# First MLP layers as Strassen block products over batches of 1024 tokens, with layer 2 added up in SBUF and attention two pairs at a time

## The reference

```python
q, k, v = x @ Wq, x @ Wk, x @ Wv
attn = softmax(q k^T * V ** -0.5)
attn_out = (attn @ v) @ Wp + bp
cms_out = gelu(attn_out @ cW1 + cb1) @ cW2 + cb2 + one_hot(target_codes, V)
modifier = gelu(concat([attn_out, cms_out]) @ mW1 + mb1) @ mW2 + mb2
x = clip(x + cms_out + modifier, 0, 1)
# expert e = stream[b] of each sequence
h = gelu(x @ W_down[e] + b_down[e]) @ W_up[e] + b_up[e] + x
out = layernorm(h) * ln_w[e] + ln_b[e]
```

## Time and profile before

| | us |
|---|---|
| median of 3 runs | 1153.08 |
| lowest, highest | 1152.85, 1154.77 |
| span of the profiled execution | 1152.9 |

### The profile page before, as it was taken

One profiled execution on the slowest core, in us unless ns is written; L12 is line 12 of the kernel. 1 busy time (PEld: TensorE's weight loads), 2 busy tenths in 40 slices (PEclk: granted clock), 3 DMA queues, 4 the chain that ended last, 5 costly groups with the idle time before them and its releaser, 6 DMA issues.

```text
span 1152.9 us, 14949 instructions
## 1 busy us (share of the span) xinstructions
PE 1119.0 (97%) x5273; PEld 935.2 (81%) x5273; DVE 519.2 (45%) x741; ACT 458.4 (40%) x739; POOL 126.2 (11%) x92
## 2 busy tenths in 40 slices
PE   8999999999999999999999999899999999899996
PEld 7888877888897887888888888688889788688885
DVE  4443354323566335322467434532346733624337
ACT  4354452333443443332444444333336244424432
POOL 1000031000005005000003201300000500500002
PEclk9999998999999998999999999999999999999999
DMA  6402354552113235473110335346311232553310
GB/s 220 172 30 92 109 174 117 185 181 81 48 36 109 78 116 151 146 254 109 55 55 9 118 106 173 96 138 243 100 36 55 71 113 76 170 137 107 104 44 37
DMA packets 135314, 128.30 MB, mean 111 GB/s; under 512 B 5950, under 2 KB 106362, under 8 KB 133242
## 3 DMA queue, kind: packets, MB, share of 16 engines
q1 hardware_dynamic: 132832, 120.61, 32.9%
q0 software_dynamic: 2368, 7.35, 1.8%
q10 hardware_dynamic: 90, 0.02, 0.0%
HBM read 119.57 MB, written 8.39 MB: 111 GB/s over the span
## 4 chain that ended last, share of the span: by engine, by line
PE 83%; issue 10%; DVE 4%; ACT 1%; POOL 1%; DVEq 0%; POOLq 0%; DMA 0%; ACTq 0%
PE bank L172 28%; PE bank L174 27%; PE bank L173 27%; DVE w_lo L616 1%; DVE hid_lo L616 1%; POOL rstd L909 1%; DVE aw_lo L616 1%; PE bank L384 0%; ACT aw_hi L511 0%; DVEq L78 0%; DVE stat L725 0%; ACT gel L446 0%; DVE x_lo L616 0%; DVE ya_lo L616 0%; DMA x_raw<-in_L_cond_Wq 0%
## 5 line engine op out<-in xcount | busy, mean ns | idle before, releaser
L616 DVE TENSOR_TENSOR w_lo<-w_raw,w_hi 128x512 fp32r<-128x512 f32 (+1 forms) x256 | 233.3, 927 | 128.2 <-ACT w_hi L437 113.8
L616 DVE TENSOR_TENSOR hid_lo<-gel,hid_hi 128x512 fp32r<-128x512 f32 x128 | 105.9, 827 | 397.9 <-ACT gel L446 397.7
L445 ACT ACTIVATE hid_hi<-bank,bias 128x512 fp32r<-128x512 f32 x128 | 88.3, 690 | 406.6 <-PE bank L174 406.6
L172 PE MATMUL bank<-hid_hi,w_lo 128*128 128x512 f32 x512 | 202.6, 396 | 15.1 <-DVE hid_lo L616 15.1
L172 PE MATMUL bank<-ya_hi,w_lo 128*128 128x512 f32 x512 | 200.8, 392 | 3.3 <-DVE w_lo L616 3.3
L173 PE MATMUL bank<-hid_hi,w_hi 128*128 128x512 f32 x512 | 202.0, 395 | 0.0
L174 PE MATMUL bank<-hid_lo,w_hi 128*128 128x512 f32 x512 | 201.9, 394 | 0.0
L174 PE MATMUL bank<-ya_lo,w_hi 128*128 128x512 f32 x512 | 200.0, 391 | 0.0
L173 PE MATMUL bank<-ya_hi,w_hi 128*128 128x512 f32 x512 | 199.8, 390 | 0.0
L437 ACT ACTIVATE w_hi<-w_raw 128x512 fp32r<-128x512 f32 x128 | 81.3, 635 | 159.7 <-PE bank L174 159.7
L172 PEld LDWEIGHTS bank<-hid_hi,w_lo 128*128 128x128 f32 x512 | 97.4, 190 | 38.7 <-DVE hid_lo L616 12.9
(11 more groups left out here) (151 smaller groups left out, 1257.0 us busy)
## 6 DMA issues: line engine op xcount, KB each, us to landing
w_raw<-in_L_cond_cW SPq DMA_DIRECT2D x128, 256.0 KB, 2.7
w_raw<-in_L_cond_mW SPq DMA_DIRECT2D x64, 512.0 KB, 4.3
w_raw<-in_L_cond_mW SPq DMA_DIRECT2D x64, 256.0 KB, 4.5
aw_hi<-proj_hi SPq DMA_DIRECT2D x6, 1024.0 KB, 7.0
aw_lo<-proj_lo SPq DMA_DIRECT2D x6, 1024.0 KB, 8.9
x_raw<-in_x SPq DMA_DIRECT2D x4, 1024.0 KB, 7.7
proj_hi<-aw_hi SPq DMA_DIRECT2D x2, 1024.0 KB, 6.0
proj_lo<-aw_lo SPq DMA_DIRECT2D x2, 1024.0 KB, 8.0
```

Of the source, the lines that this page charges most:

```text
L172: nc.tensor.matmul(dst, w_lo, a_hi, start=start, stop=False, **kw)
L445: nc.scalar.activation(hid_hi[:, q % 2, :], ps[4 + q][:, :], ACT.Gelu, bias=b)
L616: sub = lambda dst, a, hi: nc.vector.tensor_tensor(dst, a, hi.bitcast(F32), ALU.subtract)
```

## The change

Two pairs make a batch b of 1024 tokens; there are two batches. A step of the MLP is a quad, 256 hidden columns by 1024 tokens, and a batch has 24 quads in three phases of eight: phase 0 is cW1 on the attention output, phase 1 mW1's upper half on the attention output (no layer 2: its combinations, 1 MB a quad, are stored in DRAM as pre_d), phase 2 mW1's lower half on cms, to which pre_d is loaded back and added. In a quad the 512 inputs, the 256 columns and the 1024 tokens are each cut in two, and layer 1 is the seven block products of Strassen (in Winograd's form), p1 to p7, each of two `mm3` with 512 columns. Sums of weight blocks, S1 to S4, are formed on VectorE for each quad (`dve_s`) and split with A11, A12, A22 (w1_first: A11, A12, S1, S2; w1_second: A22, S3, S4; 1792 elements for high and low each); sums of token blocks, T1 to T4, once for each phase input, and split with B11, B21, B22 (`dve_t_sum`, `act_t`, `dve_t`, 1024 elements each).

ScalarE copies p1, p1+p6 and p5 out of PSUM (s1, s2, s5; in phase 2 VectorE adds them to pre: `dve_s_pre`), VectorE adds to them (c11, c22, c12 in `dve_c`), c21 is copied by ScalarE; then Gelu and hid. Quads overlap: in iteration `it` TensorE takes p1, p2, p5, p6 of quad it, p7, p4, p3 of quad it-1 and, between them, eight steps (six matmuls each) of layer 2 of quad it-2, in banks 6 and 7, which VectorE adds into `acc` in SBUF one by one (`dve_evac`). Iterations 0, 1 and 10 to 17 have no layer 2. POOL keeps only the powers of the layer norm (four columns in one); `dve_resid` adds x to acc in iteration 15, in two instructions of 2048 elements.

Attention takes both pairs of a batch one behind the other, x being copied twice by ScalarE (xf, x_hi). The expert of a batch (`pe_expert`, both pairs, down, residual and up) comes behind the next batch's attention, or at the end. Its weights come in eight pieces of 1024 elements for a batch (`load_piece`) through two buffers of `e_raw`, which are the same bytes as `w1_raw`: SyncE loads piece k when piece k-2 is split, and W1 of quad 0 of the next batch when piece 6 is split. ScalarE's order at the second entry (`act_attention`) is VectorE's below: pieces 0, 1, xp, pieces 2, 3, ao of the first pair, B11, B21, ao of the second, T1, expert down of the first pair, pieces 4, 5, xp, T2, pieces 6, 7, w1_first, T3, B22, down of the second pair, T4. All loops are unrolled.

```diff
+        def pe_mlp(pe, b):
+            def l1(i, bank, w, t, start):
+                hi, lo = (tc_hi, tc_lo) if phase_of(i) == 2 else (ta_hi, ta_lo)
+                which = phase_of(i) // 2
+                if i in (0, 1, 2 * NQ, 2 * NQ + 1):
+                    pe.wait_ge(t_lo, 14 * b + 7 * which + T_NO[t] + 1)
+                for k in range(2):
+                    last = mm3(ps[3 * (i % 2) + bank][:, :], w1_hi[:, i % 2, W_NO[w], k, :],
+                               w1_lo[:, i % 2, W_NO[w], k, :], hi[:, T_NO[t], k, :], lo[:, T_NO[t], k, :],
+                               start and k == 0, k == 1, skip_group_check=True)
+                return last
+            def first(i, which):
+                g = quad(b, i)
+                if which == 1:
+                    pe.wait_ge(w1_l1, 3 * g + 2)
+                    if i >= 2:
+                        pe.wait_ge(c21_done, g - 1)
+                    elif b == 0:
+                        pe.wait_ge(ao_done, 8)
+                    else:
+                        pe.wait_ge(z_sum, 4 * (i + 1))
+                    l1(i, 0, "A11", "B11", True).then_inc(p1_mm, 1)
+                elif which == 2:
+                    if i >= 2:
+                        pe.wait_ge(c11_done, g - 1)
+                    l1(i, 1, "A12", "B21", True).then_inc(p2_mm, 1)
+                elif which == 5:
+                    pe.wait_ge(w1_l1, 3 * g + 3)
+                    if i >= 2:
+                        pe.wait_ge(c12_done, g - 1)
+                    l1(i, 2, "S1", "T1", True).then_inc(p5_mm, 1)
+                else:
+                    pe.wait_ge(s1_done, g + 1)
+                    l1(i, 0, "S2", "T2", False).then_inc(p6_mm, 1)
+            def second(i, which):
+                g = quad(b, i)
+                if which == 7:
+                    pe.wait_ge(w1_l2, 2 * g + 2)
+                    pe.wait_ge(s2_done, g + 1)
+                    l1(i, 0, "S3", "T3", False).then_inc(p7_mm, 1)
+                elif which == 4:
+                    pe.wait_ge(c22_done, g + 1)
+                    l1(i, 0, "A22", "T4", False).then_inc(p4_mm, 1)
+                else:
+                    pe.wait_ge(s5_done, g + 1)
+                    l1(i, 2, "S4", "B22", False).then_inc(p3_mm, 1)
+            def l2(i, k):
+                r = l2_of(b, i)
+                reg, slot = phase_of(i) // 2, r % 2
+                t, j = divmod(k, KT)
+                if k == 0:
+                    pe.wait_ge(w2_l, r + 1)
+                    pe.wait_ge(hid_l["11"], r + 1)
+                    pe.wait_ge(hid_l["21"], r + 1)
+                elif k == KT:
+                    pe.wait_ge(hid_l["12"], r + 1)
+                    pe.wait_ge(hid_l["22"], r + 1)
...
+                for c in range(2):
+                    w = slice(j * P, (j + 1) * P)
+                    last = mm3(ps[6 + k % 2][:, :], w2_hi[reg][:, slot, c, w], w2_lo[reg][:, slot, c, w],
+                               hid_hi[reg][:, slot, c, t, :], hid_lo[reg][:, slot, c, t, :], c == 0, c == 1)
+                last.then_inc(l2_mm, 1)
+            for it in range(QB + 2):
+                new, old, dn = it < QB, 0 <= it - 1 < QB, has_l2(it - 2)
+                if it == QB + 1 and b + 1 < NBAT:
+                    pe_tr(pe, 2 * b + 2, 0)
+                for step, which in enumerate((1, 2, 7, 5, 6, 4, 3)):
+                    if which in (1, 2, 5, 6):
+                        if new:
+                            first(it, which)
+                    elif old:
+                        second(it - 1, which)
+                    if dn:
+                        l2(it - 2, step)
+                if dn:
+                    l2(it - 2, 7)
...
+        def act_mlp(act, b, tail):
+            cms_t = {10: ("B11", "B21"), 11: ("T1",), 12: ("T2", "T3"), 13: ("B22",), 14: ("T4",)}
+            for it in range(QB + 2):
+                new, old = it < QB, 0 <= it - 1 < QB
+                ph, pph = phase_of(it), phase_of(it - 1)
+                if new:
+                    act_w1_second(act, b, it)
+                    if ph < 2:
+                        act_s(act, b, it, 1)
+                if it + 1 < QB:
+                    act_w1_first(act, b, it + 1, 0)
+                if new and ph != 1:
+                    act_gelu(act, b, it, "11")
+                if it + 1 < QB:
+                    act_w1_first(act, b, it + 1, 1)
+                if old and pph != 1:
+                    act_gelu(act, b, it - 1, "22")
+                    act_hid(act, b, it - 1, "22")
+                if new and ph < 2:
+                    act_s(act, b, it, 5)
+                if old and pph != 1:
+                    act_w2(act, b, it - 1)
+                if new and ph < 2:
+                    act_s(act, b, it, 2)
+                if old:
+                    if pph == 1:
+                        act_c21_copy(act, b, it - 1)
+                    else:
+                        act_gelu(act, b, it - 1, "21")
+                        act_hid(act, b, it - 1, "21")
+                for name in cms_t.get(it, ()):
+                    act_t(act, b, 1, name)
+                if new and ph != 1:
+                    act_hid(act, b, it, "11")
+                if old and pph != 1:
+                    act_gelu(act, b, it - 1, "12")
+                    act_hid(act, b, it - 1, "12")
...
+        def dve_s(dve, b, i):
+            g = quad(b, i)
+            a11, a12, a21, a22 = raw_blocks(i)
...
+            dve.wait_ge(w1_in[i % 2], 16 * (g // 2) + 16)
+            nc.vector.tensor_tensor(s_f[:, 0, :, :], a21, a22, ALU.add).then_inc(s_step, 1)
+            nc.vector.tensor_tensor(s_f[:, 2, :, :], a11, a21, ALU.subtract).then_inc(s_step, 1)
+            dve.wait_ge(s_step, 4 * g + 1)
+            nc.vector.tensor_tensor(s_f[:, 1, :, :], s_f[:, 0, :, :], a11, ALU.subtract).then_inc(s_step, 1)
+            dve.wait_ge(s_step, 4 * g + 3)
+            nc.vector.tensor_tensor(s_f[:, 3, :, :], a12, s_f[:, 1, :, :], ALU.subtract).then_inc(s_step, 1)
...
+        def dve_s_pre(dve, b, i, which):
+            g = quad(b, i)
+            landed, bank, tile, done = {1: (p1_mm, 0, 0, s1_done), 2: (p6_mm, 0, 1, s2_done),
+                                        5: (p5_mm, 2, 2, s5_done)}[which]
+            dve.wait_ge(pre_in[i % 3], 16 * in_count(b, i))
+            dve.wait_ge(landed, g + 1)
+            dst = sbc[:, i % 3, tile, :]
+            nc.vector.tensor_tensor(dst, ps[3 * (i % 2) + bank][:, :], dst, ALU.add).then_inc(done, 1)
...
+        def dve_c21_pre(dve, b, i):
+            dve.wait_ge(p4_mm, quad(b, i) + 1)
+            dst = sbc[:, i % 3, 3, :]
+            nc.vector.tensor_tensor(dst, ps[3 * (i % 2)][:, :], dst, ALU.add).then_inc(c21_done, 1)
+        def dve_c(dve, b, i, key):
+            g = quad(b, i)
+            first, landed, bank, tile, done = {"11": (s1_done, p2_mm, 1, 0, c11_done),
+                                               "22": (s5_done, p7_mm, 0, 2, c22_done),
+                                               "12": (s2_done, p3_mm, 2, 1, c12_done)}[key]
+            dve.wait_ge(first, g + 1)
+            dve.wait_ge(landed, g + 1)
+            dst = sbc[:, i % 3, tile, :]
+            nc.vector.tensor_tensor(dst, ps[3 * (i % 2) + bank][:, :], dst, ALU.add).then_inc(done, 1)
...
+        def dve_attention(dve, b):
...
+            dve_softmax(dve, n)
+            dve_tiles(dve, v_h, 4 * n, 4, lambda k: vv_hi[:, 0, k, :], lambda k: vv_lo[:, 0, k, :], v_l)
+            dve_softmax(dve, n + 1)
+            dve_tiles(dve, v_h, 4 * n + 4, 4, lambda k: vv_hi[:, 1, k, :], lambda k: vv_lo[:, 1, k, :], v_l)
+            dve_probs_T(dve, n)
+            dve_probs_T(dve, n + 1)
+            if b:
+                dve_expert_piece(dve, b - 1, 0)
+                dve_expert_piece(dve, b - 1, 1)
+                dve_xp(dve, 2 * b - 2)
+                dve_expert_piece(dve, b - 1, 2)
+                dve_expert_piece(dve, b - 1, 3)
+            dve_t(dve, b, 0, "B11")
+            dve_t(dve, b, 0, "B21")
+            if b == 0:
+                dve_s(dve, b, 0)
+            dve_t_sum(dve, b, 0, "T1")
+            dve_t_sum(dve, b, 0, "T2")
+            dve_t(dve, b, 0, "T1")
+            if b:
+                dve_h3(dve, 2 * b - 2)
+                dve_expert_piece(dve, b - 1, 4)
+                dve_expert_piece(dve, b - 1, 5)
+                dve_xp(dve, 2 * b - 1)
+            dve_t_sum(dve, b, 0, "T3")
+            dve_t(dve, b, 0, "T2")
+            if b:
+                dve_z(dve, 2 * b - 2)
+                dve_expert_piece(dve, b - 1, 6)
+                dve_expert_piece(dve, b - 1, 7)
+                dve_s(dve, b, 0)
+            dve_w1_first(dve, b, 0)
+            dve_t(dve, b, 0, "T3")
+            dve_t_sum(dve, b, 0, "T4")
+            dve_t(dve, b, 0, "B22")
+            if b:
+                dve_h3(dve, 2 * b - 1)
+                dve_norm(dve, 2 * b - 2)
+                dve_z(dve, 2 * b - 1)
+            dve_t(dve, b, 0, "T4")
+            if b:
```

(136 more changed lines are left out.)

1577 lines of the change are left out of this document (830 added, 747 removed).

## The result

| | before | after |
|---|---|---|
| median, us | 1153.15 | 1193.05 |
| lowest, highest | 1152.85, 1154.77 | 1191.55, 1194.39 |
| span of the profiled execution | 1152.9 | 1191.9 |
| mean granted TensorE clock | 0.989 | 0.958 |

The ratio is 1.034, with a 95% interval from 1.0326 to 1.0355: slower by 3.4%. The forecast was 1174.0, range 1128 to 1203.

A forecast was written before the change was run, and what follows sets the result against it. TensorE's instruction stream was taken to bound the kernel. Its remaining work of 1028.4 us plus seven losses (8.0, 3.3, 18.1, 9.0, 41.4, 31.9, 34.0) gave 1174.1 us, range 1128 to 1203.

The forecast's parts named there:

- What is taken away: Layer 1 loses 288 matmuls, 65.3 us; the 25.3 us lost at the MLP's four phase edges behind POOL's additions go.
- TensorE's own work: Whole kernel: matmul time without waits, 1093.7 us before, less 65.3, is 1028.4 us.
- Totals covered with layer 2: MLP quads with layer 2: TensorE's 20.4 us covers VectorE's 13.8 (16.2 in phase 2) and ScalarE's about 11; no wait.
- Loss 1: Prologue: y starts at about 37.0 where work is 29.0, one more ScalarE copy than before; 8.0 us.
- Loss 2: Attention's own waits, for transposes and x_l of the second pair, evac and x_lo at the second batch; 3.3 us.
- Loss 3: First entry to the MLP: VectorE's fixed order of T sums and splits delays p1 of quads 0 and 1; 18.1 us.
- loss 4: Iterations 10 to 15: late T copies and splits delay c12, then c22, so p4 waits; 4.5 a batch, 9.0 us.
- loss 5: Iterations 16 to 18: pre's load stands behind a store waiting for c12; 20.7 a batch with low clock, 41.4 us.
- The load's landing: Pre's load for quad 16, behind the store, lands 6.0 us after issue, against 3.9 for a first transfer.
- Loss 6: Second entry: VectorE's 57.1 us of expert, norm and T work plus about 11.6 of waits delays quad 1; 31.9 us.
- Loss 7: Tail: one chain of pieces, reloads, expert, norms and store takes 60 us where TensorE's work is 26; 34.0 us.
- The rival of the lower ends: Whole kernel: chains cost only VectorE's summed instructions, other waits overlap, pre lands early; 1110.7 us, chance 0.17.

The follow-up runs named there:

- all five orders: The changed kernel with pre's load ahead of the store, T copies early, and first entry, second entry and tail reordered: 1137.64 us, ratio 0.985.

## Why the prediction was right, and where it was 18 us short

The direction and its reason held: 288 matmuls and the phase edges went, and more was lost in new waits at the places named. By its steps, times from TensorE's rows:

- **What is taken away**: 24.2 measured for the edges' 25.3; matmuls still start 0.227 apart. The 65.3 is TensorE's work; through the waits of after it was worth 44.0.
- **TensorE's own work**: 1028.4 is 7.2 too little. The row of sixteen residual matmuls, 1.79, is half a pair's: the sixteen of the program stand as 32 in the trace, 3.6 us, so an expert part is 14.8, not 13.0. The sum still holds, because losses 6 and 7 were reckoned as end times less the same 13.0 a pair; as waits they are 3.6 smaller each, and of the 59.2 lost in before 7.2 are work.
- **Totals covered with layer 2**: held. From the first to the last layer-2 product of phase 0 it is 161.5 us in both batches, where 711 starts of 0.2267 make 161.2.
- **Loss 1**: first y at 38.22, forecast 37.0.
- **Loss 2**: 3.2, forecast 3.3.
- **Loss 3**: V, the end of the last values product, is 96.1; p1 of quad 0 at V + 25.3, forecast V + 25.4, of quad 1 at V + 34.5, forecast 34.4. The 2.5 that the sum adds for the low clock did not come on top of that: the clock was low only before quad 1 (0.73 granted up to 130.6, 1.00 from there to 144.6). In its place came waits that the prediction does not have, in iteration 1: 1.36 for c22 of quad 0 and 0.95 for its c21, which ScalarE makes with its Gelu (the row at 143.13), so that p1 of quad 2 starts 12.5 us after p1 of quad 1, not 9.5. That the size came within 0.8 of the forecast is luck.
- **Losses 4 and 5**: the middle takes 106.2 and 109.0, where its work is 78.2 (345 starts): 58.7 lost, 50.4 forecast. Mechanism and places held: four gaps, ended by s1 and c22 behind a load. Two terms were mis-sized. Iterations 11 to 15 (loss 4) lost 6.0 a batch for 4.5. Iterations 16 and 17 lost 21.2 and 24.3, for 14.2 and the 4 of the clock, and there it is the clock: some 7.9 and 7.4 by busy time against the kernel with all five orders. Of the 2.5 for hid_lo in iteration 18 only 0.8 and 0.5 came.
- **The load's landing**: 6.9 and 8.4 at the first of a batch, for the 6.0 taken. The 6.0 and the 3.9 beside it are the two quickest transfers of a view that holds stores too, and both are stores of the prologue. The 1024 KB loads of before landed 6.5 to 7.8 us after their issue, those right behind another one 7.6 to 9.8.
- **Loss 6**: p1 of quad 1 at V + 78.0 (V is 622.1), forecast V + 76.6 with its clock; layer 2 4.5 later than the sum has it. The 3.1 of that in iteration 1 are the low clock of its first matmuls (0.43 apart up to 703.2) and again the wait for c21, 0.99. The size held. That it is made by VectorE's sum, with the second pair's h3 behind it, fits the two runs there (less work gave half, another order next to nothing), but isn't shown by them.
- **Loss 7**: 59.3 after the last layer-2 matmul, forecast 60.
- **The shortfall.** Above the forecast lie 1.2 (loss 1), 0.8 (loss 3), 8.3 (losses 4 and 5), 4.5 (loss 6), 0.6 in the two layer-2 stretches of phase 0 and 3.1 in those of phase 2 (150.1 and 147.2, where the work is 148.0 and 146.2); below it 0.1 (loss 2) and 0.5 (loss 7). That is 17.9, and the spans differ by 17.8 (1191.9, 1174.1).

The prediction named two rules of the Trainium skill. That of the page TensorE: Matmul & The Clock Gate (Part 1: The HAM clock gate), an idle array at half rate that only sustained work lifts, bears more than the 13 us given to it: 7.9 and 7.4 in the two middles alone, at a clock of 0.90 and 0.89 against 0.99 and 0.98. That of DMA: Bandwidth & Descriptors (Queues, rings and completion order), one queue's descriptors taken in ring order by each DMA engine, agrees with the loads of quad 16, which landed 2.0 and 2.8 us sooner once the store stood behind them. That is 4.8 in all, not the 8 of the prediction.

The rival of the lower ends needed loss 5 under 25 and the entries and tail together under 60, and had neither. The kernel with all five orders, 1137.6 on the same instructions, shows that 55 us of what kept it away was the order of the work. The 27 that are left to the rival's 1110.7 no order tried here removed.

## What to carry to other kernels

Price a saved product by what the bound engine will do with the time: here 65 us of matmuls was worth 44, and in the two stretches without layer 2 a third of itself and next to nothing, until the orders of three other engines were changed. Write down for each engine that executes in a fixed order what stands ahead of the one result TensorE waits for, DMA issues too: one exchanged pair of DMA issues was worth 26 us. Where moving work doesn't shorten a stretch, take work out of it as a probe; if that gives only part, look for a second chain.
